# Counting edges of a graph kernel two targets at a time, in 16-bit words

## The reference, cut to what matters

```python
agg = jax.ops.segment_sum(x[src], dst, num_segments=N)   # twice in L0, twice in L3
h = (1.0 + eps) * x + agg                                # L0
```

## Time and profile before

| | |
|---|---|
| median of three runs | 3587.89 us |
| the profiled execution, its own time | 3585.43 us |
| its span, first to last instruction | 3584.1 us |
| the counting, first key one-hot to last add | 20.49 to 315.38 us |
| mean granted TensorE clock | 0.823 |

### The profile page before, as it was taken

One profiled execution on the slowest core, in us unless ns is written; L12 is line 12 of the kernel. 1 busy time (PEld: TensorE's weight loads), 2 busy tenths in 40 slices (PEclk: granted clock), 3 DMA queues, 4 the chain that ended last, 5 costly groups with the idle time before them and its releaser, 6 DMA issues.

```text
span 3584.1 us, 57380 instructions
## 1 busy us (share of the span) xinstructions
PE 2579.5 (72%) x12616; PEld 1659.6 (46%) x12616; DVE 1998.7 (56%) x3057; ACT 1526.7 (43%) x3452; POOL 2009.4 (56%) x1999
## 2 busy tenths in 40 slices
PE   4887976766667565666986565569965556599898
PEld 1334445555555344444654343446644444366444
DVE  8886764444445444446964444459844444588211
ACT  8674443333334333334743333337633333367211
POOL 0000007777763777776747777768667777677000
PEclk7999987677878777668996877769987777799999
DMA  2002026555544878875968887849678888578200
GB/s 72 0 1 115 1 67 201 162 169 163 168 114 140 263 262 262 261 261 170 327 214 261 262 263 260 263 136 319 240 255 260 264 263 263 181 276 287 116 1 18
DMA packets 271543, 679.40 MB, mean 190 GB/s; under 512 B 48513, under 2 KB 81206, under 8 KB 270038
## 3 DMA queue, kind: packets, MB, share of 16 engines
q1 hardware_dynamic: 156758, 336.25, 28.4%
q0 software_dynamic: 73216, 190.95, 18.4%
q10 hardware_dynamic: 41472, 151.01, 11.1%
HBM read 502.07 MB, written 175.94 MB: 189 GB/s over the span
## 4 chain that ended last, share of the span: by engine, by line
POOL 36%; PE 32%; issue 16%; DMA 6%; DVE 5%; ACT 3%; DVEq 2%; POOLq 1%; ACTq 0%; SPq 0%
POOL region L414 19%; POOL tN L414 17%; PE psum L490 9%; PE psum L741 9%; PE psum L504 5%; DMA region<-tab,idx_ring 3%; PE psum L706 2%; PE psum L580 2%; PE psum L721 2%; DMA tN<-tab,idx_ring 1%; DVE acc L1453 1%; DVEq L1088 1%; ACT psum L1809 1%; DMA region<-tabs,idx_ring 1%; DVE region L1092 1%
## 5 line engine op out<-in xcount | busy, mean ns | idle before, releaser
L934 PE MATMUL psum<-w_all,region 128*128 128x256 f32 x2496 | 913.7, 534 | 632.6 <-ACT region L1795 611.6
L934 PEld LDWEIGHTS psum<-w_all,region 128*128 128x128 f32 x2496 | 642.9, 269 | 903.0 <-issue 714.0
L414 POOL DMA_INDIRECT region<-tab,idx_ring x624 | 591.5, 948 | 319.3 <-issue 314.4
L414 POOL DMA_INDIRECT tN<-tab,idx_ring x624 | 590.1, 946 | 190.2 <-issue 182.2
L414 POOL DMA_INDIRECT region<-tabs,idx_ring x208 | 206.7, 994 | 588.6 <-issue 586.7
L1942 POOL TENSOR_TENSOR region<-node_no,dst_rel 128x256 f32<-128x256 f32 x312 | 413.6, 1326 | 137.4 <-ACT region L1839 112.6
L1461 DVE TENSOR_TENSOR tN<-tN,psum 128x1024 f32<-128x1024 f32 x156 | 190.5, 1221 | 417.8 <-DMA tN<-tab,idx_ring 409.5
L1453 DVE TENSOR_TENSOR acc<-acc,psum 128x1024 f32<-128x1024 f32 x312 | 379.1, 1215 | 46.2 <-ACT psum L1809 46.1
L1461 DVE TENSOR_TENSOR region<-region,psum 128x1024 f32<-128x1024 f32 x156 | 190.4, 1220 | 377.9 <-DMA region<-tab,idx_ring 356.0
L1809 ACT ACTIVATE psum<-region 128x1024 f32<-128x1024 f32 x156 | 160.2, 1027 | 439.5 <-DVE acc L1453 280.5
L1809 ACT ACTIVATE psum<-tN 128x1024 f32<-128x1024 f32 x156 | 160.2, 1027 | 402.9 <-DVE acc L1453 402.9
(11 more groups left out here) (310 smaller groups left out, 3470.9 us busy)
## 6 DMA issues: line engine op xcount, KB each, us to landing
region<-e_t SPq DMA_DIRECT2D x416, 256.0 KB
pre_dram<-region ACTq DMA_DIRECT2D x144, 512.0 KB, 3.6
pre_dram<-tN ACTq DMA_DIRECT2D x144, 512.0 KB, 3.9
region<-pre_dram SPq DMA_DIRECT2D x144, 512.0 KB, 5.0
tN<-pre_dram SPq DMA_DIRECT2D x144, 512.0 KB, 5.0
tA<-dst_row SPq DMA_DIRECT2D x78, 256.0 KB
adj_kept<-region SPq DMA_DIRECT2D x5, 2000.0 KB, 16.9
region<-adj_kept SPq DMA_DIRECT2D x5, 2000.0 KB, 17.0
```

Source lines behind the costliest of these rows:

```text
L414: pool.indirect_dma_start(m_ring[j][:, c, at:at + width], None, table[:, :], bass.IndirectOffsetOnAxis(ap=idx_at(j, k)[:, c:c + 1], axis=0 ...
L934: mm = pe.matmul(banks[:, 2 * (j % 2) + c // 2, (c % 2) * 256:(c % 2) * 256 + 256], e_ring[:, j % E_SLOTS, c * D:(c + 1) * D], W(f"ee{l}") ...
```

## The change

Two neighbouring targets are counted in one 16-bit word. The window is 24 targets, 12 words: its start is made even, the key is tile x 12 + (target >> 1) - start/2, and the one-hot holds 1 for an even and 256 for an odd target (`weight`), so that adding as int16 adds to the right byte. One-hots, matmuls and adds have 25 x 12 = 300 columns, not 500. Ring slots shrink accordingly. The check no longer asks that no lane count is above 15.5: it caps each at 15.25, sums them all, and asks that the sum reaches the number of edges.

```diff
-ADJ_WIN = 20
-ADJ_COLS = ADJ_WIN * N_TILES
+ADJ_WIN = 24
+ADJ_PAIRS = ADJ_WIN // 2
+ADJ_COLS = ADJ_PAIRS * N_TILES
+        pairs = region.bitcast(I16)[:, :].rearrange("p (t d) -> p t d", t=N_TILES)
-        key, lane = (flat_n[:, NP + k * NG * GC:NP + (k + 1) * NG * GC] for k in range(2))
+        key, lane, weight = (flat_n[:, NP + k * NG * GC:NP + (k + 1) * NG * GC] for k in range(3))
+            even = small[0:NG, 32:34].bitcast(I32)
+            dve.wait_ge(v.sem, v.did(dve.tensor_copy(even, ends[:, 0:2])))
+            dve.wait_ge(v.sem, v.did(dve.tensor_scalar(even, even, -2, None, ALU.bitwise_and)))
+            dve.wait_ge(v.sem, v.did(dve.tensor_copy(ends[:, 0:2], even)))
...
-            dve.wait_ge(v.sem, v.did(dve.tensor_scalar(ends[:, 0:2], ends[:, 0:2], line, None, ALU.max)))
+            dve.wait_ge(v.sem, v.did(dve.tensor_scalar(ends[:, 0:2], ends[:, 0:2], line, 0.5, ALU.max, ALU.mult)))
...
+            v.did(dve.tensor_scalar(odd_i, dst_i, 1, None, ALU.bitwise_and))
             dve.wait_ge(v.sem, v.did(dve.tensor_scalar(tile_i, src_i, D.bit_length() - 1, None, ALU.arith_shift_right)))
-            dve.wait_ge(v.sem, v.did(dve.tensor_copy(tile_f, tile_i)))
-            dve.wait_ge(v.sem, v.did(dve.scalar_tensor_tensor(out=tile_f, in0=tile_f, scalar=float(ADJ_WIN), in1=neg,
+            v.did(dve.tensor_copy(weight, odd_i))
+            dve.wait_ge(v.sem, v.did(dve.tensor_scalar(dst_i, dst_i, 1, None, ALU.arith_shift_right)))
+            v.did(dve.tensor_copy(tile_f, tile_i))
+            dve.wait_ge(v.sem, v.did(dve.tensor_copy(key, dst_i)))
+            v.did(dve.tensor_scalar(weight, weight, 255.0, 1.0, ALU.mult, ALU.add))
+            dve.wait_ge(v.sem, v.did(dve.scalar_tensor_tensor(out=tile_f, in0=tile_f, scalar=float(ADJ_PAIRS), in1=neg,
                                                               op0=ALU.mult, op1=ALU.subtract)))
-            dve.wait_ge(v.sem, v.did(dve.tensor_tensor(key, tile_f, dst_rel[:, :], ALU.add)))
+            dve.wait_ge(v.sem, v.did(dve.tensor_tensor(key, tile_f, key, ALU.add)))
...
-                    to = counts[:, :, bass.ds(start, ADJ_WIN)]
+                    to = pairs[:, :, bass.ds(start, ADJ_PAIRS)]
...
                             last = dve.tensor_scalar(key_ring[j % KEY_SLOTS][:, c, :], key_no,
-                                                     key[:, bass.ds(g * GC + c, 1)], None, ALU.is_equal)
+                                                     key[:, bass.ds(g * GC + c, 1)], weight[:, bass.ds(g * GC + c, 1)],
+                                                     ALU.is_equal, ALU.mult)
...
-                dve.wait_ge(v.sem, v.did(dve.tensor_scalar(check_out[:, lo:hi], deg_lane[:, lo:hi], MAX_COUNT + 0.5, 0.0,
-                                                           ALU.is_le, ALU.add, accum_out=over_sum[:, n:n + 1])))
-            dve.wait_ge(v.sem, v.did(dve.tensor_tensor(small[:, 14:15], over_sum[:, 0:1], over_sum[:, 1:2], ALU.add)))
-            dve.tensor_scalar(small[:, 14:15], small[:, 14:15], NP - 0.5, None, ALU.is_lt).then_inc(S["bad_lane"], 1)
+                dve.wait_ge(v.sem, v.did(dve.tensor_scalar(check_out[:, lo:hi], deg_lane[:, lo:hi], MAX_COUNT + 0.25, 0.0,
+                                                           ALU.min, ALU.add, accum_out=over_sum[:, n:n + 1])))
+            dve.tensor_tensor(small[:, 14:15], over_sum[:, 0:1], over_sum[:, 1:2], ALU.add).then_inc(S["bad_lane"], 1)
...
+            dve.wait_ge(v.sem, v.did(dve.tensor_scalar(complete, x_ps[0:1, 0:1], N_EDGES - 0.1, -1.0, ALU.is_ge, ALU.mult)))
+            dve.tensor_tensor(irregular[:, :], complete, small[0:1, 12:13], ALU.add).then_inc(S["irregular_set"], 1)
```

More of the change, by code:

```diff
@@ L13 @@
 I8 = mybir.dt.int8
+I16 = mybir.dt.int16
 ALU = mybir.AluOpType
@@ L261, in build @@
         scratch = flat_n[:, 0:NP]
-        key, lane = (flat_n[:, NP + k * NG * GC:NP + (k + 1) * NG * GC] for k in range(2))
-        at_ = NP + 2 * NG * GC
+        key, lane, weight = (flat_n[:, NP + k * NG * GC:NP + (k + 1) * NG * GC] for k in range(3))
+        at_ = NP + 3 * NG * GC
         key_no = flat_n[:, at_:at_ + ADJ_COLS // 2].bitcast(FP16)
@@ L1044, in dve_program @@
             v.did(dve.tensor_copy(far, x_ps[:, 384:385]))
-            v.did(dve.tensor_copy(small[0:1, 12:13], x_ps[0:1, 385:386]))
+            v.did(dve.tensor_scalar(small[0:1, 12:13], x_ps[0:1, 385:386], 1.0, None, ALU.add))
             dve.wait_ge(v.sem, v.did(dve.tensor_scalar(node_col_i[:, :], node_col_i[:, :], WIN - 1, None, ALU.bitwise_and)))
@@ L1054, in dve_program @@
             last.then_inc(S["setup_to_pe"], 1)
-            lane_i, tile_i = scratch[:, 2048:2048 + NG * GC].bitcast(I32), src_i
+            lane_i, tile_i, odd_i = scratch[:, 0:NG * GC].bitcast(I32), src_i, scratch[:, 512:512 + NG * GC].bitcast(I32)
             tile_f = scratch[:, 1440:1440 + NG * GC]
@@ L1087, in add_counts @@
                 for k in range(2):
-                    start = dve.value_load(adj_at_i[0:1, bass.ds(2 * g + k, 1)], min_val=0, max_val=N_NODES - 1)
-                    to = counts[:, :, bass.ds(start, ADJ_WIN)]
+                    start = dve.value_load(adj_at_i[0:1, bass.ds(2 * g + k, 1)], min_val=0, max_val=N_NODES // 2)
+                    to = pairs[:, :, bass.ds(start, ADJ_PAIRS)]
                     dve.wait_ge(S["adj_mm"], T["adj_mm"] + 2 * g + k + 1)
@@ L1129, in dve_program @@
                 dve.wait_ge(S["deg_sum"], N_FIRST - 1 + n)
-                dve.wait_ge(v.sem, v.did(dve.tensor_scalar(check_out[:, lo:hi], deg_lane[:, lo:hi], MAX_COUNT + 0.5, 0.0,
-                                                           ALU.is_le, ALU.add, accum_out=over_sum[:, n:n + 1])))
-            dve.wait_ge(v.sem, v.did(dve.tensor_tensor(small[:, 14:15], over_sum[:, 0:1], over_sum[:, 1:2], ALU.add)))
-            dve.tensor_scalar(small[:, 14:15], small[:, 14:15], NP - 0.5, None, ALU.is_lt).then_inc(S["bad_lane"], 1)
+                dve.wait_ge(v.sem, v.did(dve.tensor_scalar(check_out[:, lo:hi], deg_lane[:, lo:hi], MAX_COUNT + 0.25, 0.0,
+                                                           ALU.min, ALU.add, accum_out=over_sum[:, n:n + 1])))
+            dve.tensor_tensor(small[:, 14:15], over_sum[:, 0:1], over_sum[:, 1:2], ALU.add).then_inc(S["bad_lane"], 1)
             dve.wait_ge(S["bad_mm"], 1)
-            dve.wait_ge(S["bad_mm"], 1)
-            dve.tensor_tensor(irregular[:, :], x_ps[0:1, 0:1], small[0:1, 12:13], ALU.add).then_inc(S["irregular_set"], 1)
+            complete = small[0:1, 34:35]
+            dve.wait_ge(v.sem, v.did(dve.tensor_scalar(complete, x_ps[0:1, 0:1], N_EDGES - 0.1, -1.0, ALU.is_ge, ALU.mult)))
+            dve.tensor_tensor(irregular[:, :], complete, small[0:1, 12:13], ALU.add).then_inc(S["irregular_set"], 1)
             dve.wait_ge(S["irregular_set"], 1)
```

## The result

The changed kernel takes 3595.1 us (median of 16 runs, 3588.75 to 3604.36); the kernel before, run beside it, 3584.11 us (16 runs, 3576.54 to 3591.75). The ratio is 1.0031, interval 1.0024 to 1.0038: **11.0 us slower**. The forecast had +7.7 us, with 0.52 on slower by over 0.2%, a median of 3595.6 us and a range from 3583 to 3609. That 3595.6 lies only 0.5 us from the measured median is luck: the forecast started from 3587.89, the median of three runs, which is 3.8 above that of 16, and the change was forecast 3.3 too small.

The account below looks back on a forecast made before the run. VectorE's sequencer was taken to bound the looped trips. Trips 0 and 1 -9.0, loop addresses +19.4, stalls -4.7, setup +2.2, last add -0.2 summed to +7.7 us on 3587.9: 3595.6 us, range 3583 to 3609.

Parts of the forecast that it names:

- Which engine bounds the loop: In the 11 looped trips VectorE's sequencer sets the pace at 2.64 us a group; its engine would do with 2.49.
- Adds: 208 VectorE adds go from 500 to 300 columns: 472 ns each, 0.205 us less, worth nothing inside the loop.
- The rival worked out beside it: VectorE's engine is the bound in the loop after all, every group gains 0.62 us: 3532 us; chance 0.03.
- Keys: Four VectorE key one-hots of a group go from 1.03 to 0.83 us; gain only in trips 0 and 1.
- The 0.9 that the trips' ends were to take back: At ends of trips 0 and 1, four adds in a row meet the sequencer's 0.82 us: 0.9 of 9.9 lost.
- Trips 0 and 1 as the engine's own: In the constant-address trips VectorE's engine is the bound, 2.49 us a group, shortened by 0.62: -9.0 us.
- Loop address work: In the loop, the second key operand's counter-dependent address and the window's address add 0.22 us a group: +19.4 us.
- The rival of an instruction for each address: In the loop each key address takes its own sequencer instruction: +32 us, sum +20, 3608 us; chance 0.14.
- that of a free second address: In the loop the second key address costs nearly nothing: +1 instead of +19.4, sum -9, 3579 us; chance 0.13.
- Stalls: VectorE's waits for late TensorE in looped trips, 7.1 us in all, mostly vanish: -4.7 us (0 to -7.1).
- Setup: Before VectorE's first key, five added 128x416 operations and three tiny ones, with nothing hiding them: +2.2 us.
- TensorE's clock: Rival: TensorE drops to half clock in the loop, once a trip costing 8 instead of 2.4 us: 3601; chance 0.08.

Follow-up runs that it names:

- e1: The changed kernel with its key one-hot taking immediate 1.0 instead of the `weight` operand, so odd targets' counts land on even ones; ratio to the kernel before 0.9976.
- e6: The changed kernel with the bounds of a window's start stated at build time instead of tested at run time; ratio to the kernel before 0.9946.
- e9: The kernel before with keys copied to a fixed tile once a looped trip and window starts not tested at run time; 3571.64 us, ratio 0.9966.
- e10: The changed kernel with keys and weights copied to a fixed tile once a looped trip and starts not tested at run time; 3535.34 us, ratio 0.9867.
- e7: The changed kernel as it is, run again beside others on one chip; ratio to the kernel before 0.999 to 1.0031, given as 1.001.

## Why the prediction was right

The right view was that the sequencer bounds the loop. By its steps:

- **Which engine bounds the loop**: shown. e1 removes 0.61 us of engine work a group and gains nothing in the loop; e6 takes sequencer work out that its expectation put at 0.26 us twice a group, and a group gets 0.56 shorter.
- **Adds**, forecast 472 ns: 470. The Trainium skill, "VectorE: DVE Perf Modes", section on the TRN2 errata, gives 470 as an estimate by its (N + 151) cycles, and the trace agrees with it. The rival worked out beside it, 3532 us for the whole kernel, did not come; where the sequencer was relieved, the shorter adds paid in full (e9 against e10).
- **Keys**, forecast 0.83 for four, range named with "a second per-partition operand costs each key some 0.06": this is the term that was **mis-sized**. Four take 1.08 in the changed kernel (keys from 49.38, next add 50.46) and 0.84 in e1. 0.83 was right for one operand; the 0.06 that I left in the range was real. Trips 0 and 1 gave 5.95, not 9.0: 16 groups at 0.37 instead of 0.62. The 0.9 that the trips' ends were to take back is there (adds 0.82 apart), but about as much came in at their starts, where TensorE had held VectorE up by 0.36 and 0.33 before a trip's first add (23.01 and 47.49 in the kernel before) and no longer does.
- **Trips 0 and 1 as the engine's own**: not quite. e9's looped group of 2.42 shows that 0.07 of their 2.49 was the sequencer's.
- **Loop address work**, forecast 0.22 a group, +19.4: undisturbed trips grew by 1.84, 0.23 a group, 20.2 over 11. The line was misread for its smallest part: L1090 holds a wait's value and stays at 40 ns (L1104 now); the window's address is at L1092, 40 ns, and became 46 to 50 (L1106). The size, 0.01 a group, was right. The address has 93 ns as expected ("near 90"), and the spilled operation is there, 40 ns, once a group. The rival of an instruction for each address fell with the row of L1115 (316 fused instructions for 316 keys), that of a free second address with its 93 ns.
- **Stalls**, forecast -4.7 of 7.1: 11 trips of 23.55 are 259.05 of 261.17, so 2.1 are left, -5.0. Before, five trips were 1.0 to 2.5 us over 21.71; now four are 0.3 to 0.9 over 23.55. That the term came out so near is in part luck: in e7's profile of the same kernel 4.1 are left.
- **Setup**, forecast +2.2: the first key is 1.65 later. The added operations take 2.06 (the setup's last one starts at 21.03, before at 18.97), but the idle before the first key is 1.05 where it was 1.46. That gain of 0.41 I had not foreseen, and its cause is not settled.
- **TensorE's clock**: nothing that reached the time. Granted 0.95 in the looped part before and after.

The window from 22 to 67 us, changed kernel and kernel before:

```profile
22.00:67.00 45.00, 18.77 (x66) 7.27 (x67) 39.86 (x107) 41.89 (x96) 0.00 (x0) 1.00 0.00 1
```

```profile
22.00:67.00 45.00, 24.47 (x64) 6.68 (x62) 40.14 (x94) 40.97 (x94) 0.00 (x0) 0.73 0.00 1
```

There the granted clock is higher with the short matmuls, 1.00 against 0.73. But the matmuls themselves don't run faster. TensorE's timeline of the changed kernel, four matmuls of 300 columns in trip 1 and four in the loop:

```profile
59.31 1.16 PE L725 MATMUL psum<-deg,tN 128*128 128x300 bf16 x4 [0.97 <-DVE deg L1115]
...
113.99 0.68 PE L725 MATMUL psum<-tN 128*128 128x300 bf16 x4 [3.31 <-DVE tN L1115]
```

The difference, 0.12 us a matmul or 0.4 ns a column, is that between the clock's two levels, 1.2 and 2.4 GHz. So in trips 0 and 1 the matmuls of the changed kernel go at the lower level throughout, while in the kernel before some groups' four go at the higher one (1.01 us) and some at the lower (1.83). Read the matmuls' own lengths beside the granted clock. The loss costs little there: no add of an ordinary group waits for TensorE, one at a trip's end does (0.72 us, at 39.14).

The measured terms are +1.65 - 5.95 + 15.27 = +10.97; the forecast of the same three was +2.2 - 9.0 + 14.5. Nearly all of the 3.3 us to +7.7 is the 3.05 of trips 0 and 1, which is the keys.

## What to carry to other kernels

When an engine's busy time falls and the stage grows, look at the sequencer's own rows: in a loop with dynamic addresses each vector instruction costs its address arithmetic, and an operand added to it costs more of that. Halve the engine's work only after the sequencer has been relieved, by copying a trip's scalars to a fixed place and by not testing at run time what the data guarantee; the same change cost 11 us without that and gained 36 us with it. Sum the cost of a second per-partition operand both in the sequencer and in the engine.

## What the runs showed of the hardware

- The second per-partition operand makes a tensor_scalar 60 ns longer at 300 columns (294 to 354) and at 500 (345 to 406).
- In a fused register instruction an operation costs about 11 to 12 ns: 46, 57 and 93 ns for what the source makes two, three and six operations. The first key address of a group, with more to work out, took up to 105 ns and a plain instruction of 40 beside it; where exactly the limit of one instruction lies is not shown.
- A register load with run-time bounds costs the sequencer 0.30 + 0.19 + 0.02 us and the gaps; without the test 0.28 us less, by the distance of the adds (1.01 to 0.73).
- Two dependent adds on VectorE stand 0.12 us more than their length apart when nothing else in the profile holds them (0.59 for 0.47, 0.80 for 0.68), and 0.19 to 0.21 more where a wait and an address instruction stand between them (trips 0 and 1).
- TensorE's granted clock in the profile and the rate of its matmuls can differ: 1.00 for 22 to 67 us of the changed kernel, with four matmuls of 300 columns in 1.16 us, against 0.68 later.
